# Key operands loaded ahead of x, all early steps between the projections, and the first queries' loads begun from ScalarE's queue

## The reference

```python
q = (x @ wq).reshape(B, S, 16, 16); k, v = (x @ wk), (x @ wv)   # 4 key/value heads
q = q * cos + rotate_half(q) * sin; k = k * cos + rotate_half(k) * sin
attn = softmax(q k^T / sqrt(16)); x = layernorm(x + (attn v) @ wo)
h = silu(x @ Wg.T) * (x @ Wu.T);  x = layernorm(x + h @ Wd.T)
```

## Time and profile before

| | us |
|---|---|
| median of 3 runs | 902.25 (901.34 to 904.5) |
| the profiled execution | 899.15, its span 897.3 |
| PE busy | 881.7 (98%) |
| DVE busy | 741.9 (83%) |
| ACT busy | 712.9 (79%) |
| POOL busy | 268.6 (30%) |
| mean granted TensorE clock | 0.989 |
| chain that ended last, by engine | PE 89%, DVE 4%, ACT 2%, issue 2%, DMA 1%, SPq 1% |

### The profile page before, as it was taken

The page is one execution under the profiler, slowest core; times in us unless marked ns, Lnnn a source line. Parts: engine busy times, 40 slices in busy tenths (PEclk is TensorE's granted clock), DMA queues, the critical chain, the costliest instruction groups (busy, mean ns, idle before and its releaser), DMA issues.

```text
span 897.3 us, 16216 instructions
## 1 busy us (share of the span) xinstructions
PE 881.7 (98%) x5658; PEld 460.2 (51%) x5658; DVE 741.9 (83%) x1655; ACT 712.9 (79%) x929; POOL 268.6 (30%) x232
## 2 busy tenths in 40 slices
PE   9999999999999999999999999999999999999996
PEld 3334444444444444444444444444436888888885
DVE  5577999999999999999999999999955455665545
ACT  2467999999999999999999999999985566555564
POOL 7763430035434000001001000210104665665555
PEclk9997999999999999999999999999999999999998
DMA  8973553323443132232223313121112010110001
GB/s 265 295 205 113 130 123 79 90 81 77 99 124 61 45 77 64 56 73 67 52 54 85 73 46 78 45 67 32 37 55 57 25 48 24 48 47 25 24 24 48
DMA packets 53458, 69.98 MB, mean 78 GB/s; under 512 B 17344, under 2 KB 26560, under 8 KB 53376
## 3 DMA queue, kind: packets, MB, share of 16 engines
q1 hardware_dynamic: 50280, 65.53, 28.4%
q0 software_dynamic: 864, 3.15, 1.2%
q10 hardware_dynamic: 2232, 0.25, 0.2%
HBM read 46.74 MB, written 16.25 MB: 70 GB/s over the span
## 4 chain that ended last, share of the span: by engine, by line
PE 89%; DVE 4%; ACT 2%; issue 2%; DMA 1%; SPq 1%; POOL 0%; POOLq 0%; DVEq 0%; ACTq 0%
PE pv_bank L1374 26%; PE ring_bank L1286 24%; PE pair_bank L1432 13%; PE pair_bank L1500 12%; PE pv_bank L1526 3%; PE ring_bank L1526 3%; PE ring_bank L1384 2%; PE pair_bank L1320 2%; DVE block_max L851 2%; ACT probs L1187 1%; DMA q_parts<-low 1%; PE ring_bank L1399 1%; PE pv_bank L1338 1%; DVE above L847 0%; PE pv_bank L1264 0%
## 5 line engine op out<-in xcount | busy, mean ns | idle before, releaser
L1187 ACT ACTIVATE probs<-pair_bank 128x1024 f32<-128x1024 f32 x512 | 495.7, 1023 | 43.2 <-PE pair_bank L1432 43.1
L851 DVE TENSOR_REDUCE block_max<-ring_bank 128x1 f32<-128x384 f32 x854 | 486.7, 609 | 15.4 <-PE ring_bank L1286 6.0
L1286 PE MATMUL ring_bank<-k_max,q_sb 48*128 48x512 f32 x1127 | 313.3, 445 | 1.8 <-DVE block_max L847 0.7
L1286 PEld LDWEIGHTS ring_bank<-k_max,q_sb 48*128 48x128 f32 x1127 | 150.2, 185 | 267.5 <-DVE block_max L851 116.8
L1374 PE MATMUL pv_bank<-probs,v_all 128*17 128x512 f32 x2048 | 270.5, 600 | 0.6 <-ACT probs L1187 0.5
L1432 PE MATMUL pair_bank<-q_sb,k_sb 50*128 50x512 f32 x1024 | 221.5, 428 | 1.2 <-ACT probs L1187 0.7
L1042 DVE SCALAR_TENSOR_TENSOR hid<-pair_bank,up_s,silu 128x512 f32<-128x512 f32 x63 | 47.1, 748 | 85.0 <-ACT silu L1243 85.0
L1432 PEld LDWEIGHTS pair_bank<-q_sb,k_sb 50*128 50x128 f32 x1024 | 99.1, 186 | 29.5 <-ACT probs L1187 7.4
L760 POOL TENSOR_TENSOR hid_l<-hid,hid_h 128x512 fp32r<-128x512 f32 x63 | 81.7, 1297 | 86.3 <-ACT hid_h L1222 85.6
L675 POOL TENSOR_TENSOR attn<-attn,inv_rows 128x1024 f32<-128x1024 f32 x7 | 16.7, 2388 | 300.8 <-DMA inv_rows<-inv_d 228.5
L847 DVE CUSTOM_DVE_ANT_0 above<-ring_bank,above 128x512 f32<-128x512 f32 x137 | 94.0, 688 | 5.7 <-PE pair_bank L1286 3.6
(11 more groups left out here) (142 smaller groups left out, 862.0 us busy)
## 6 DMA issues: line engine op xcount, KB each, us to landing
k_max<-k_parts SPq DMA_DIRECT2D x96, 96.0 KB, 3.6
q_sb<-q_parts SPq DMA_DIRECT2D x64, 128.0 KB, 3.4
k_sb<-k_parts SPq DMA_DIRECT2D x96, 64.0 KB, 2.3
attn<-xT SPq DMA_DIRECT2D x8, 512.0 KB, 5.4
q_parts<-high SPq DMA_DIRECT2D x16, 256.0 KB, 3.7
q_parts<-low SPq DMA_DIRECT2D x16, 256.0 KB, 4.1
q_sb<-q_parts SPq DMA_DIRECT2D x64, 64.0 KB, 3.5
attn<-pv_sb SPq DMA_DIRECT2D x128, 32.0 KB
```

What stands on the lines that cost most here:

```text
L851: dve.reduce_max(block_max[half % 2][:, col:col + 1], bank[:, 0:width], axis=AX.X).then_inc(ring_used, 1)
L1187: act.activation(probs[t % 2][:, 2 * pr:2 * pr + 2, :], pair_bank[pr][:], ACT.Exp, scale=D ** -0.5).then_inc(probs_ready, 1)
L1286: pe.matmul(bank[:, 0:last - first], q_sb[k][rows, i, qt * P:(qt + 1) * P], k_max[k // QH][rows, kind * CH + first:kind * CH + last], star ...
```

## The change

- **Early steps.** Step i now lies in hook 28 + i * 20 // 24, so 24 steps fill the 20 hooks from (4, 4) to (7, 5), and hooks 28, 33, 38 and 43 have two. Nothing comes between the projections and the loop. The ring has three banks throughout (`WIDE_BANKS` is gone). The last batch element's values are turned in unit 1 of the loop; ScalarE copies their rows after unit 0's second exponential, and the product of unit 0 waits for that copy.
- **SP in block 2.** Gap high part, queries' high part, gap low part, then `first_keys` (wait for the stores of keys and gap, six key loads), then x of block 5, the queries' low part, the second group.
- **ScalarE in block 2.** `gap_high` goes ahead of the high part (2, 0). Between the high parts (2, 0) and (2, 1) ScalarE waits for the stores of blocks 0 and 1 and begins the four loads of the first queries (`first_queries`).
- **Low part of the first keys** is made by VectorE after `rotary_q(2, 1)` instead of by GpSimd between the two rotations of block 2.
- **Shift.** SP's `load_shift(0, 0)` moves from ahead of block 7's stores to between the stores of block 6's first and second group; GpSimd's wait for the shift from low(7, 0) to low(6, 0).
- **Loop start.** In unit 0 scores come first, mixed with the maxima, instead of after them; ScalarE takes unit 0's "above" after its first exponential.

```diff
-VALUES_BEHIND = 8
-VALUES_COPIED = 1
-KEYS_COPIED = 5
-WIDE_BANKS = 5
+FIRST_STEP = 28
+VALUES_UNIT = 1
...
         for i in range(2 * LEAD):
-            n, h = divmod(FIRST * HOOKS + i, HOOKS)
-            where = early[(n, h) if n < BLOCKS else (BLOCKS, HOOKS - 1)]
-            where.extend(step(i))
-        early[BLOCKS, HOOKS - 1].insert(VALUES_BEHIND, ("v", B - 1))
...
+            early[divmod(FIRST_STEP + i * (BLOCKS * HOOKS - FIRST_STEP) // (2 * LEAD), HOOKS)].extend(step(i))
...
+            if g == VALUES_UNIT:
+                place(("v", B - 1), "v")
...
         def bank_index(pos):
-            return early_place(pos) if pos < early_entries else (0, 1, 2 * BANKS)[pos % BANKS]
+            return (0, 1, 2 if pos < early_entries else 2 * BANKS)[pos % BANKS]
...
-            def first_loads():
-
-                for slot in range(4):
-                    sp.wait_ge(stored[slot], 16 * 2)
-                load_q(0, 0, sp)
+            def first_keys():
+
                 sp.wait_ge(k_stored[0], 16 * 2)
                 sp.wait_ge(gap_stored, 16 * 2)
                 sp.wait_ge(memsets, 6)
                 load_k(k_max, 0, 0, kmax_loaded, sp)
...
-                    if last and c == 1:
+                    if m == 2:
+                        store_gap(0, (0,))
+                        store_q(m, 0, (0,))
+                        store_gap(0, (1,))
+                        first_keys()
+                        load_x(m + 3)
+                        store_q(m, 0, (1,))
+                    else:
+                        store_q(m, 0)
+                        if m + 3 < BLOCKS:
+                            load_x(m + 3)
+                    if last and c == 0:
                         load_shift(0, 0)
-                    store_q(m, 0)
-                    if m == 2:
-                        store_gap(0)
-                    if m + 3 < BLOCKS:
-                        load_x(m + 3)
-                    if m == 2:
-                        first_loads()
                     store_q(m, 1)
...
-                if m == BLOCKS - 1 and j == 0:
+                if m == BLOCKS - 2 and j == 0:
                     after_turn(0)
...
                 rotate(m, 0)
-                if m == 2:
-                    low_of_k(0)
                 rotate(m, 1)
...
                 rotary_q(m, 1)
+                if m == 2:
+                    low_first_k()
...
+            def first_queries():
+
+                for slot in range(4):
+                    act.wait_ge(stored[slot], 16 * 2)
+                load_q(0, 0, act)
...
+                if m == 2:
+                    gap_high()
                 high_part(m, 0)
                 early_takes(m, 4)
+                if m == 2:
+                    first_queries()
                 high_part(m, 1)
                 early_takes(m, 5)
-            for h in range(HOOKS):
-                early_takes(BLOCKS, h)
+            copy_k_rows(B - 1)
...
+                            if (g, pr) == (0, 0):
+                                difference(*maxima_at(g))
+                            if (g, pr) == (0, 1):
+                                copy_v_rows(B - 1)
+                            if (g, pr) == (VALUES_UNIT, 1):
+                                take_v(B - 1)
...
+                if g == 0:
+                    pe.wait_ge(v_rows_ready, B)
...
                         if first and k == 0 and t == 0:
-                            for i in range(len(entries)):
+                            scores(0)
+                            maxima(0)
+                            maxima(1)
+                            scores(1)
+                            for i in range(2, len(entries)):
                                 maxima(i)
-                            scores(0)
-                            scores(1)
...
+                        if g == VALUES_UNIT:
+                            transpose_v(B - 1)
```

More of the change, by code:

```diff
@@ L248, in step @@
             return [(half, 4 * t + 2 * (i % 2) + r) for r in range(GROUPS)]
-        early = {(n, h): [] for n in range(BLOCKS + 1) for h in range(HOOKS)}
+        early = {(n, h): [] for n in range(BLOCKS) for h in range(HOOKS)}
         for b in range(B):
@@ L318, in last_in @@
         def last_in(index, pos):
-            return max((p for p in range(max(pos - 2 * BANKS - 2, 0), pos) if bank_index(p) == index), default=None)
+            return max((p for p in range(max(pos - BANKS, 0), pos) if bank_index(p) == index), default=None)
         last_reader = {}
@@ L407, in store_q @@
                 cols = slice(c * CH, (c + 1) * CH)
-                for part, buf, ready, count in ((0, high, hi_ready, 2 * m + j + 1), (1, low, lo_ready[j], m + 1)):
+                for part, buf, ready, count in [((0, high, hi_ready, 2 * m + j + 1), (1, low, lo_ready[j], m + 1))[q] for q in parts]:
                     sp.wait_ge(ready, count)
@@ L417, in store_k, with store_gap @@
                     sp.dma_start(k_parts[b, part, 0:QH].rearrange("c r t -> (c r) t"), buf[:].bitcast(fp32)).then_inc(k_stored[b], 16)
-            def store_gap(b):
-                for part, buf, ready in ((0, gap_h, gap_h_ready), (1, gap_l, gap_l_ready)):
+            def store_gap(b, parts=(0, 1)):
+                for part, buf, ready in [((0, gap_h, gap_h_ready), (1, gap_l, gap_l_ready))[q] for q in parts]:
                     sp.wait_ge(ready, b + 1)
@@ L1359, in _ @@
             early_work(BLOCKS - 1, HOOKS - 1)
-            for h in range(HOOKS):
-                early_work(BLOCKS, h)
             pe.wait_ge(parts_ready, Q_PARTS * BLOCKS)
-            pe.wait_ge(v_rows_ready, B)
-            pe.wait_ge(v_used, 2 * B)
             pe.wait_ge(memsets, 6)
@@ L1421, in scores @@
                             if first and k == 0 and t == 0:
[L1422 to L1423 removed]
+                                if pr:
+                                    pe.wait_ge(*taken(last_in(BANKS - 1, early_entries)))
                             else:
```

32 lines of the change are left out of this document (8 added, 24 removed).

## The result

The changed kernel is slower. Its median over 22 runs is 907.39 us (901.85 to 910.0), against 902.19 us (900.4 to 909.28) for 22 runs of the kernel before on the same chips; the ratio is 1.0033, with a 95% interval of 1.0016 to 1.0049. The forecast was 898.8 (896.3 to 904.3) and a gain. The medians lie 5.2 us apart and the ratio says 3.0; both kernels scatter by eight to nine, and the ratio with its interval is the figure to go by. The profiled execution of the changed kernel took 908.72 (span 906.9) and is one of the slower ones; that of before, 899.15, is faster than any of its 22 timed ones. The two traces are therefore 9.57 apart, three times what the ratio says: what follows explains a slow execution of the changed kernel against a fast one of before, and how much of it holds for the rest is read from the ratios of the experiments.

A forecast was written before the change was run, and what follows sets the result against it. TensorE, nearly always busy, was taken as the bound, losing time only in waits or at a halved clock. The second unit pair starting at 78.5 instead of 81.9 gave -3.4 us: median 902.25 to 898.8, range 896.3 to 904.3.

The forecast's parts named there:

- pv(2): Product of unit 2, start of the loop's second unit pair: forecast at 78.5 instead of 81.94, the end moving with it.
- The gap's store and the keys: SP, block 2: low gap stored at 25.5, landing 2.6 to 2.9, key loads from 28.4, last landed at 34.5.
- Rival C: Front chain ends on the DMA side: TensorE waits at step 1 for late landings; 904.5 us, chance 0.15.
- ScalarE's query loads: Block 2: wait ends at 25.8, four issues take 1.9 us, block 4's key and value products come 1.2 late.
- The low store: Block 2's low query part, queued behind key loads: out at 31.8, landed after 4.5 at 36.3, block 5 starts at 37.9.
- The clock in the projections: Within rival C: with a wait of four microseconds the clock can fall inside the projections, 2 us more.
- The doubled hooks: Four hooks with two steps: in blocks 5 to 7 a second step adds 0.43 us and a stall of 0.5 each.
- The moved shift and the moved low key part: Shift stores on SP from about 59.8 to 64.3, low key part on VectorE: both forecast to cost nothing.
- The loop's start: Last "above" pair at 67.5, product of unit 0 at 73.6, pv(2) at 78.5, at the full clock.
- rival B: Clock falls anyway at the loop's start from short bank waits: pv(2) at 81.5, total 902.1, no change; chance 0.25.
- A: The main forecast, clock staying up at the loop's start: around 898.8 us (896.5 to 901); chance 0.50.
- Rival D: Waits only change places: bank waits in the hooks and ScalarE's later high parts take the gain; 901 to 902, chance 0.10.

The follow-up runs named there:

- e4: The changed kernel with the first queries' four loads issued by SP instead of ScalarE; 906.28 us, ratio 1.0044 to the kernel before.
- e6: The changed kernel with the low store ahead of the key loads and the four query loads on SP; 906.1 us, ratio 1.0027 to before.
- e1: The kernel before with only the change's new order of loads and stores in block 2; 904.78 us, ratio 1.0032.
- e5: The changed kernel with the low store of block 2's first queries moved ahead of the key loads; 903.32 us, ratio 1.0007 to before.
- e7: The changed kernel with unread products filling TensorE's waits, three before block 4's keys and values, two before the fourth maxima block; 904.18 us, ratio 1.001 to before.
- e10: e6 with three unread full products ahead of the first maxima step; 902.45 us, ratio 0.9981 to the kernel before.
- e8: The kernel before with a small unread product (128 columns) after each of the tail's twelve maxima blocks; 914.21 us, ratio 1.011.
- e2: The changed kernel with the old order of loads in block 2; 906.45 us, ratio 1.0048 to the kernel before.
- e3: e2 with the early steps starting at hook 30, six hooks doubled instead of four; 906.97 us, ratio 1.0067 to the kernel before.
- e9: e6 with the early steps starting at hook 30 instead of 28; 907.41 us, ratio 1.0039 to the kernel before.
- e13: e10 with unit 0 of the loop in its old order, all five maxima blocks before the scores; 904.19 us, ratio 1.0006 to the kernel before.

## Why the prediction was wrong

It failed by 11.75 us at pv(2): 90.25 against 78.5. Of this, 1.4 is the late start of that execution. The rest goes down the prediction's own terms in order.

**The gap's store and the keys: mis-sized, 1.9 us at the start of the key loads and 2.9 at their landing.** Forecast were the low gap's store at 25.5, a landing of 2.6 to 2.9 and key loads at 28.4. Taken back by the 1.4 of the start, it went out at 25.65, as forecast, but landed after 4.5, and the loads started at 30.25. The landing was read from the earlier trace rows, taken where the query loads came later. In the new order the query loads that ScalarE sends share its time: without them beside it the landing is 3.6 and 3.9 (e4, e6). The keys' own landing, 4.9 for the last one, is also above the 3.5 to 4.2 of the earlier trace rows, so they had landed at 38.8 - 1.4 = 37.4 instead of 34.5. Rival C had a price for this, "1 us more for the gap's", and it was 1.6 to 1.9. The Trainium skill (DMA: Bandwidth & Descriptors, Issuing engines are not separate DMA queues) says that transfers begun from several engines share the same DMA engines, so that a second queue is no second lane. The runs agree, with 3.6 to 3.9 against 4.4 to 5.3. Even the longest of the gap's own rows, 2.9, was too short; only the queries' stores had rows of this length (2.8 to 7.2).

**ScalarE's query loads: mis-sized.** The wait ended at 27.15 - 1.4 = 25.75, as forecast (25.8). The issues took 3.05, not 1.9: 0.76 for one in the mean, where 0.51 was taken from the one issue of ScalarE in the earlier trace rows. In the other profiles with this order the four took 2.3 to 2.8 (e1, e5, e7). The slack behind it was put at 0.5, and TensorE's wait came to 2.50 where 1.2 was forecast.

**The low store: the step that failed.** It was forecast to go out at 31.8 and to land after 4.5, at 36.3. It went out at 34.84 - 1.4 = 33.4, because the key loads it is queued behind were late, and landed after 5.7, at 39.1. The prediction had the chain complete, store of the gap, keys, block 5's input, low store, high(4,0), "above", and had its direction right. It priced each link by rows in which the link stood in lighter traffic; the same store had landed after 2.8 in its old place, at 26.56 in the kernel before. Moving this one store takes the ratio from 1.0033 to 1.0007 (e5), and mending the other alone leaves it at 1.0044 (e4): this chain ended last. How much of e5's gain is the wait (2.24 to 0.45) and how much the clock that stayed up with it, e5 alone doesn't part; e6, without either cause and still at 1.0027, shows that the clock is a large part of it. Together, block 5 started at 42.55 - 1.4 = 41.15 against a forecast of 37.9: 3.25 us of the miss.

**The clock in the projections: foreseen as a possibility, and not weighed.** Rival C had it in half a sentence ("with a wait of four microseconds the clock can fall inside the projections too"), for 2 us. Blocks 5 to 7 took 34.8 us; in e10, at the full clock, 70.29 - 39.70 = 30.6, and 29.6 was forecast: 4.2 for the low clock and 1.0 for the rest. The prediction took its guide from the earlier trace rows, where the clock had stayed up around 36 us with TensorE busy for 0.54 of one microsecond. That row said what such a wait did in one execution, and no more. In the runs of before, too, the longest executions are among those with the lowest mean clock (910.43 us at 0.983, 900.82 at 0.992).

**The doubled hooks: mis-sized by 1.0.** TensorE's stalls in those of blocks 5 to 7 are short in e10, 0.22, 0.27 and 0.38, where 0.5 was forecast. But from the pair of 47.08 to the next product, at 48.69, the doubled hook takes 1.61, and the single one 0.43 (45.64 to 46.07): a second step costs 1.18, not 0.43 + 0.5, and in the other two hooks 1.18 and 1.36, 3.7 in all for 2.8.

**The moved shift and the moved low key part: right, at nothing.** The shift's eight stores go out at 71.51 and take 4.94, some 12 us later than forecast (59.8 to 64.3), about as far as the front and blocks 5 to 7 are late and two more, and the first scores, at 78.77, wait for none of them. No row of TensorE shows a wait for VectorE in block 2. GpSimd waits 1.2 for the shift, and nobody waits for GpSimd there but ScalarE, 0.6 at most.

**The loop's start: mis-sized, 1.9 us.** 11.0 was forecast from the last "above" pair to pv(2), 12.9 came, and 13.8 in e10, where the clock was low for longer. Forecast was a granted clock of 1.00 from 64 to 82. The clock fell to 0.50 in this stretch in every profile of a kernel with this start, between 74.0 (e10) and 82.6 (the changed kernel). Here rival B was right in what happens; its "short waits in a row" are there in these profiles (0.57, 0.44 and 0.28 in the changed kernel), but e8 shows a fall without them. Its own terms, by the way, give 902.3 and not 902.1. The Trainium skill (TensorE: Matmul & The Clock Gate, A second HAM failure mode: psum-queue depth-cycling) blames brief idle stretches of an engine cycling through banks; e8 shows no recorded wait between 67 and 83, and the clock falls in that stretch, at 69.2, and stays low for thirty microseconds. What does decide it isn't settled by these runs.

**The gain that was to be had.** From the end of block 4 to pv(2), with the waits at the front taken out, the kernel before needs 46.2 us, e10 45.5 and e5 44.8, whose clock was low at the loop's start for 3.4 us instead of 6.8. To spread the tail over the hooks wins 0.7 to 1.5 us in these traces and not the 3.4 of the sum: the prediction counted the tail's waits and low clock as won, and the loop's start brings the low clock back.

The chances were set wrong in one place. A (0.50) rested on bounds of +3 for the landings with the middle at 0, and C, whose mechanism it was, had 0.15. The change puts more transfers into the same ten microseconds, and that was a reason to set the middle of the landings at the upper rows. The front's 3.25 alone takes the forecast from 898.8 to 902.0, no change; blocks 5 to 7 and the loop's start take it to 909.2, which is the changed kernel in its longer executions. 904.5, rival C's time, is 2.9 us below the median of the 22 runs, and 0.7 below what the ratio gives, 1.0033 times 902.19 = 905.2. So the rival with 0.15 had the chain and nearly the size, though it reached it by a landing of 7.2 where 5.7 came and by 2 us for the clock where 4.2 came. Rival D's waits that only change places (901 to 902) are what e4 shows, but the changed kernel has more of them than before, 5.12 us for 1.15.

## What to carry to other kernels

A load begun from a computing engine's queue costs that engine its wait and its issues (2.3 to 3.05 us for four here), and a store moved behind loads is paid for where its buffer is used again, two blocks on; follow both to the engine that stands behind them before the order is changed. Where transfers are packed closer, take their landings from the longest rows, not from the middle. And where TensorE must stand some microseconds between full-size products, two or three products that nobody reads are a cheap try: they took e6 from 906.1 to 902.45, and the scatter with it. It isn't a rule for every place: small products in a tail of small products took the kernel before to a ratio of 1.011 (e8).

## What the runs showed of the hardware

- The clock fell in the projections after TensorE had stood 3.6 to 5.1 us in all at the front in the profiles of e2, e3, e4, e6 and the changed kernel, and the fall cost 4.2 us in the last. It didn't fall there in the profiled execution of e9 with 4.0 in all, 3.58 of it in one piece, nor in e1 and e5 with 3.8 and 3.1 in pieces of up to 2.31. It isn't decided by the length of the wait alone.
- A TensorE that is recorded as busy without a gap from 67 to 83 us, with short products and maxima blocks in turn, had its clock fall two microseconds into that stretch, at 69.2, and had it back only at 99.9 (e8).
- Four DMA issues from ScalarE's queue took 0.38, 1.19, 0.78 and 0.61 us, and 0.36, 0.91, 0.46 and 0.46 in e1, next to 0.60, 0.51, 0.42 and 0.43 for the same four from SP's queue in e4.
- The low store of block 2's first queries landed after 2.8 us in the kernel before, where it went out at 26.56, and after 5.7 behind six key loads and block 5's input. Sent ahead of the key loads it took 5.0 (e5) and 4.6 (e6), so the place in the queue isn't all of it.
- The store of the gap's low part landed after 3.6 to 3.9 us with the four query loads behind it on SP's queue (e4, e6, e9, e10, e13), and after 4.4 to 5.3 with them sent from ScalarE's queue beside it (the changed kernel, e1, e5, e7).
